# Window attention in one pass on one core: second scores one step later, rings of seven for the maxima, softmax sums spread by VectorE

## What is computed

```python
x = conv(quantize(min(1, |x|)), sign(W) * mean|W|) + b
# attention over 7x7 = 49 regions of 8x8 = 64 tokens, 8 heads of 8, the 4 best regions for each
qkv = layernorm(x) @ wqkv + bqkv
idx = top_k(mean(q) . mean(k), 4)                     # per region
kg, vg = k[idx], v[idx]                               # 4 x 64 = 256 keys
attn = softmax(q @ kg.T / sqrt(8)) @ vg
x = x + attn @ wo + bo
x = x + gelu(layernorm(x) @ w1 + bm1) @ w2 + bm2
```

## Time and profile before

| what | value |
|---|---|
| median of 3 runs | 5555.56 us (5546.46 to 5559.63) |
| the profiled execution | 5569.85 us, its span 5568.0 us |
| mean granted TensorE clock | 0.909 |
| TensorE busy | 4677.0 us, 84% |
| VectorE busy | 3447.6 us, 62% |
| ScalarE busy | 3285.4 us, 59% |
| GpSimd busy | 2747.0 us, 49% |
| transfers | 487.33 MB in 627124 packets, 88 GB/s |

### The profile page before, as it was taken

The page is one execution under the profiler, slowest core; times in us unless marked ns, Lnnn a source line. Parts: engine busy times, 40 slices in busy tenths (PEclk is TensorE's granted clock), DMA queues, the critical chain, the costliest instruction groups (busy, mean ns, idle before and its releaser), DMA issues.

```text
span 5568.0 us, 230234 instructions
## 1 busy us (share of the span) xinstructions
PE 4677.0 (84%) x68754; PEld 3217.0 (58%) x68754; DVE 3447.6 (62%) x7969; ACT 3285.4 (59%) x6282; POOL 2747.0 (49%) x9656
## 2 busy tenths in 40 slices
PE   2388888888889888888888888888888888888888
PEld 1265565656556565565656656565565656556564
DVE  2266666666666666666666666666566666667665
ACT  1156556565665656556565665656556565665656
POOL 1245455454544545445454554545455454554553
PEclk8589999998998999889989999989899999989999
DMA  1333343333333333333333423333343333323311
GB/s 53 102 98 92 83 109 76 100 77 96 102 77 98 84 95 91 82 103 80 94 83 91 111 72 103 81 96 92 79 109 79 96 81 102 100 75 102 84 40 33
DMA packets 627124, 487.33 MB, mean 88 GB/s; under 512 B 483792, under 2 KB 613968, under 8 KB 615536
## 3 DMA queue, kind: packets, MB, share of 16 engines
q10 hardware_dynamic: 335360, 205.62, 16.4%
q1 hardware_dynamic: 290416, 265.73, 16.2%
HBM read 262.38 MB, written 208.73 MB: 85 GB/s over the span
## 4 chain that ended last, share of the span: by engine, by line
PE 45%; DMA 18%; issue 10%; SPq 7%; ACT 7%; DVE 5%; DVEq 3%; POOL 2%; ACTq 2%; POOLq 1%
DMA max_d<-tr 11%; PE ps L988 9%; PE ps L1002 7%; PE ps L1019 7%; PE ps L881 4%; DMA qm<-qk_d 3%; PE ps L938 3%; DMA xin<-in_x 3%; DVEq L223 2%; DVE mx L724 2%; SPq L327 2%; PE ps L949 2%; PE ps L901 2%; ACT hid L813 2%; PE ps L974 2%
## 5 line engine op out<-in xcount | busy, mean ns | idle before, releaser
L724 DVE TENSOR_REDUCE mx<-ps 128x4 f32<-128x1024 f32 x1568 | 1921.7, 1226 | 1702.3 <-PE ps L988 1354.0
L832 ACT ACTIVATE pt<-ps 128x512 f32<-128x512 f32 x3136 | 1694.3, 592 | 869.2 <-PE ps L1002 814.4
L506 POOL COPY vg<-vs 64x64 f32 x6272 | 1526.5, 243 | 782.0 <-POOL kg L490 576.7
L988 PE MATMUL ps<-kg,qm 96*128 96x256 f32 x6272 | 1336.2, 338 | 386.6 <-DVE mx L724 127.3
L490 POOL CAST kg<-ks 96x128 fp32r x3136 | 851.0, 297 | 1511.6 <-PE ps L1002 1156.6
L988 PEld LDWEIGHTS ps<-kg,qm 96*128 96x128 f32 x6272 | 946.8, 202 | 1053.6 <-issue 889.5
L1002 PE MATMUL ps<-qm,kg 97*128 97x256 f32 x6272 | 1119.8, 301 | 178.8 <-ACT pt L832 102.3
L1019 PE MATMUL ps<-pt,vg 128*32 128x64 f32 x50176 | 1091.4, 231 | 0.0
L1002 PEld LDWEIGHTS ps<-qm,kg 97*128 97x128 f32 x6272 | 926.2, 203 | 252.2 <-ACT pt L832 164.8
L1019 PEld LDWEIGHTS ps<-pt,vg 128*32 128x32 f32 x50176 | 826.1, 115 | 224.2 <-issue 34.8
L643 DVE CAST kg<-ks 96x128 fp32r x3136 | 625.6, 241 | 126.2 <-issue 123.5
(11 more groups left out here) (109 smaller groups left out, 3866.7 us busy)
## 6 DMA issues: line engine op xcount, KB each, us to landing
qk_d<-stg SPq DMA_DIRECT2D x224, 448.0 KB
qm<-qk_d ACTq DMA_DIRECT2D x1792, 42.0 KB
ks<-qk_d ACTq DMA_DIRECT2D x96, 784.0 KB, 6.2
vs<-v_d ACTq DMA_DIRECT2D x64, 784.0 KB, 6.7
xin<-in_x SPq DMA_DIRECT2D x119, 224.0 KB
xi_d<-xi SPq DMA_DIRECT2D x112, 224.0 KB
qk_d<-stg SPq DMA_DIRECT2D x112, 224.0 KB
max_d<-tr SPq DMA_DIRECT2D x1568, 2.0 KB
```

What stands on the lines that cost most here:

```text
L506: j = pool.tensor_copy(dst.rearrange("p j (e x) -> p j e x", e=2)[:, :, :, 0:HD], vs[place(m)[0]][rows, bass.ds(region, 1), :].rearrange(" ...
L724: v.tensor_reduce(mx[h % 2][:].rearrange("p (g j e) -> p g j e", g=2, j=2)[:, :, :, 0], ps[:, 0:2, :].rearrange("p g (j k) -> p g j k", j= ...
L832: act.activation(pt[m % 2][:, c], ps[:, 2 + c, :], ACT.Exp, scale=float(HD) ** -0.5).then_inc(S["pt_ready"], 1)
L988: i = pe.matmul(ps[:, g, 256 * j:256 * j + 256], qm[c % 2][0:NP3, t, g, 2 * j:2 * j + 2, :].rearrange("p h t -> p (h t)"), kg[slot][0:NP3, ...
```

## The change

- `ST_LAG` 3 to 4 and `PV_LAG` 4 to 5; `LEAD`, `P_AT`, `F_AT` and `ROUTE_AT` one step later. `X_AT`, `A_LOAD` and `B_LOAD` stay.
- `mx`, `tr` and `hopped` become rings of seven. VectorE's wait for a free buffer moves from the maximum to the transpose and asks for the hop of seven steps before.
- SyncE first issues the store of step h, then the read-back of step h-2.
- `pick` and its matmuls go. VectorE spreads the sums with `stream_shuffle` at offsets 0 and 1 of the finish, into `rc`, and ACT's logarithm reads `rc`. The waits that guarded PSUM banks 5 and 6 go to later matmuls.
- The queries of the next seven steps are loaded in steps 4 and 5 of each seven, four transfers each.

```diff
+SPREAD = [24] * HD + [25] * HD + [24] * 16
-ST_LAG = 3
-PV_LAG = 4
+ST_LAG = 4
+PV_LAG = 5
-LEAD = 18
+LEAD = 19
-P_AT, P_EVERY = 18, 6
-F_AT, F_EVERY = 60, 7
+P_AT, P_EVERY = 19, 6
+F_AT, F_EVERY = 61, 7
-ROUTE_AT = 62
+ROUTE_AT = 63
...
-        mx = [sb(f"mx{i}", [128, 32]) for i in range(2)]
-        tr = [sb(f"tr{i}", [128, 32]) for i in range(2)]
+        mx = [sb(f"mx{i}", [128, 32]) for i in range(RING)]
+        tr = [sb(f"tr{i}", [128, 32]) for i in range(RING)]
...
-            if t in (3, 4, 5) and live((c + 1) * NW, kind):
+            if t in (ST_LAG, ST_LAG + 1) and live((c + 1) * NW, kind):
-                if t == 3 and not (kind == "lead" and c < 1):
+                if t == ST_LAG and not (kind == "lead" and c < 1):
                     eng.wait_ge(S["st_full"], (p * STEPS + c * NW) * 2)
-                queries(eng, p + (c + 1) // 14, (c + 1) % 14, [(g, h) for g in range(NG) for h in range(HG)][(t - 3) * 3:(t - 2) * 3])
+                queries(eng, p + (c + 1) // 14, (c + 1) % 14, [(t - ST_LAG, h) for h in range(HG)])
...
-                m = h - 1
+                if live(h, kind):
+                    sp.wait_ge(S["tr_ready"], T + 1)
+                    sp.dma_start(max_d[h % RING].rearrange("j (b n) -> b j n", n=32), tr[h % RING][0:128:8, :]).then_inc(hopped[h % RING], 16)
+                m = h - 2
                 if live(m, kind):
-                    sp.wait_ge(hopped[m % 2], (p * R + m // 2 + 1) * 16)
+                    sp.wait_ge(hopped[m % RING], (p * 14 + m // RING + 1) * 16)
                     sp.dma_start(qm[m // NW % 2][NP3:NP3 + 1, m % NW].rearrange("o g h t -> o (g h t)").bitcast(F32),
                                  max_d[m % RING].rearrange("j p -> (j p)").unsqueeze(0)).then_inc(row_ready[m % RING], 16)
-                if live(h, kind):
-                    sp.wait_ge(S["tr_ready"], T + 1)
-                    sp.dma_start(max_d[h % RING].rearrange("j (b n) -> b j n", n=32), tr[h % 2][0:128:8, :]).then_inc(hopped[h % 2], 16)
...
+                    if off in (0, 1):
+                        if off == 0:
+                            v.wait_ge(S["um_ready"], p * (4 * 14) + (NW + s + 1) * 4)
+                        v.stream_shuffle(rc[:, off], um0[:, s] if off == 0 else um1[:, b], SPREAD).then_inc(S["sum_full"], 1)
...
-                    if live(h - 2, kind):
-                        v.wait_ge(hopped[h % 2], (p * R + (h - 2) // 2 + 1) * 16)
-                    v.tensor_reduce(mx[h % 2][:].rearrange(...
+                    v.tensor_reduce(mx[h % RING][:].rearrange(...
...
+                    if live(h - RING, kind):
+                        v.wait_ge(hopped[h % RING], (p * 14 + h // RING) * 16)
                     v.wait_ge(S["mx_ready"], T + 1)
-                    v.transpose(tr[h % 2][:], mx[h % 2][:]).then_inc(S["tr_ready"], 1)
+                    v.transpose(tr[h % RING][:], mx[h % RING][:]).then_inc(S["tr_ready"], 1)
...
-                        act.activation(rc[:, i], ps[:, 5 + i, 0:ST], ACT.Ln).then_inc(S["lns_ready"], 1)
+                        act.activation(rc[:, i], rc[:, i], ACT.Ln).then_inc(S["lns_ready"], 1)
...
-                    if off == 0:
-                        pe.wait_ge(S["um_ready"], p * (4 * 14) + (NW + s + 1) * 4)
-                        if s >= 2:
-                            pe.wait_ge(S["ot_ready"], 1 + n - 1)
-                        elif kind == "loop":
-                            pe.wait_ge(S["l_ready"], (p + 2) * (2 * NW))
-                            pe.wait_ge(S["v_ready"], (p + 2) * NW)
-                        if s:
-                            pe.wait_ge(S["lnv2_ready"], n)
-                        for i, src in enumerate((um0[:, s], um1[:, s % 2])):
-                            pe.matmul(ps[:, 5 + i, 0:ST], pick[:], src, start=True, stop=True).then_inc(S["sum_full"], 1)
                     if off == 4:
                         pe.wait_ge(S["un_ready"], n * 2 + 2)
                         if s:
                             pe.wait_ge(S["z_ready"], n * 2)
+                        elif kind == "loop":
+                            pe.wait_ge(S["l_ready"], (p + 2) * (2 * NW))
+                            pe.wait_ge(S["v_ready"], (p + 2) * NW)
...
                     if off == 9:
                         pe.wait_ge(S["nm2_ready"], n + 1)
-                        if s < NW - 1:
-                            pe.wait_ge(S["lns_ready"], n * 2 + 4)
+                        pe.wait_ge(S["ot_ready"], 1 + n)
+                        if s == 0 and kind == "loop":
+                            pe.wait_ge(S["lg_ready"], p + 2)
```

More of the change, by code:

```diff
@@ L110, in build @@
         ident = sb("ident", [128, 128])
-        pick = sb("pick", [128, 128])
         mean_w = sb("mean_w", [128, 128])
@@ L177, in build @@
         idx_loaded = [sem(f"idx_loaded{i}") for i in range(2)]
-        hopped = [sem(f"hopped{i}") for i in range(2)]
+        hopped = [sem(f"hopped{i}") for i in range(RING)]
         row_ready = [sem(f"row_ready{i}") for i in range(RING)]
@@ L908, in route @@
                     pe.wait_ge(S["l_ready"], q * (2 * NW) + 2 * NW)
-                    if not first:
-                        pe.wait_ge(S["lns_ready"], p * (2 * NW) + 1)
                     settled(pe)
```

17 lines of the change are left out of this document (6 added, 11 removed).

## The result

The changed kernel takes 5805.75 us in the median (5788.79 to 5838.42) against 5555.44 (5546.46 to 5559.63) of the kernel before in the same comparison: a ratio of 1.046, with a 95% interval from 1.0409 to 1.0511. It is slower by about 250 us, 16 us for each of the 16 pairs. The forecast was 5380 us and a range up to 5540; the direction was wrong.

The account below looks back on a forecast made before the run. PE was taken to bound the quiet steps, waits followed by half-clock steps the others. Terms of -0.7, -5.0, -4.5, -2.0, 0 and +1.0 made -11.2 us a pair, -176 with the ends: 5380 us, range 5250 to 5540.

Parts of the forecast that it names:

- The term of the query loads: Batches of four on ACT's queue: near nothing in quiet cycles, +1.0 us a pair in all, bounds -2 and +5.
- so it starts about 0.6 sooner: Last query batch: two more loads add 0.84 us, but no merge copy is ahead, so it starts 0.6 us sooner.
- PE idles into the low clock: Rival: without `pick`, PE's pauses in quiet cycles bring half clock, about 1.4 us more a cycle, 5540 us; chance 0.05.
- lag and order: Strip steps: read-back stalls of 6.5 us a pair against the hop wait removed; sum 0, bounds -6.7 and +9.
- the whole worth of the hop wait: The 30 strip steps: 87.3 us less 80.6 busy on PE, 6.7 us a pair, set against the read-back stalls.
- late read-back: Rival: second scores in strip items wait for the read-back, 2.8 us in each of seven items, 5590 us; chance 0.13.
- the gain in the loaded steps: Steps with key and value loads: the maximum no longer waits for a hop, -4.5 us a pair, between 0 and 8.
- about 10: The 12 steps with key and value loads: us lost a pair against the quiet pace and the loop's turn.
- the 17 later steps: Steps behind the first finish: rings give -2.0 us a pair of an excess of 8.6.
- The shuffle: VectorE's pass in place of `pick`: 0.63 us each and 0.1 for its pattern; quiet cycles -0.7 us a pair.
- The first finish: First strip's finish: the `pick` matmuls, their 2.67 us wait and slow matmuls behind leave the path, -5.0 us a pair.
- bare steps above 2.3: Sign of error: bare steps longer than 2.3 us, where the timeline before showed a cycle of 2.22.

Follow-up runs that it names:

- y2: Query loads in two batches of four, in steps 4 and 5, alone on the kernel before: 5766.19 us, ratio 1.0435.
- w1: The changed kernel with query loads 3, 3 and 2 in steps 3, 4 and 5, as before: 5629.63 us, ratio 1.0129.
- x3: The changed kernel with the `pick` matmuls back, no shuffle, and `mx` at two buffers: 5783.75 us, ratio 1.0416.
- x4: The changed kernel with unread matmuls added in the two steps that lost the `pick` matmuls: 5753.22 us, ratio 1.0369.
- v1: The changed kernel with queries 3, 3, 2 in steps 3 to 5 and the read-back of h-1 behind the store of h: 5429.32 us, ratio 0.9767.
- u2: The changed kernel with queries 3, 3, 2, read-back of h-1 behind the store, and unread matmuls in the steps without `pick`: 5360.29 us, ratio 0.9648.
- x2: Sums by shuffle in place of the `pick` matmuls, alone on the kernel before: 5489.71 us, ratio 0.9899.
- x1: Rings of seven for `tr` and `hopped`, alone on the kernel before: 5519.24 us, ratio 0.9943.
- w2: The changed kernel with queries 3, 3, 2 in steps 3 to 5 and SyncE's old order: 5480.43 us, ratio 0.9862.
- z1: Rings of seven for `tr` and `hopped` and the shuffle, together on the kernel before: 5459.52 us, ratio 0.9887.
- v2: The kernel before with rings and shuffle, and queries four and four in steps 2 and 3: 5454.74 us, ratio 0.9819.
- w3: The kernel before with rings and shuffle, and queries 3, 3, 2 a step earlier, in steps 2 to 4: 5387.11 us, ratio 0.9703.

## Why the prediction was wrong

**The term of the query loads failed most.** The sum held +1.0 a pair, bounds -2 and +5. On the kernel before the edit costs 4.35 points (y2), 15 us a pair; taking it back from the change gives 3.3 points (w1), 11.5 a pair. The step that failed is "+0.84, [...] so it starts about 0.6 sooner", which led to "near nothing in quiet cycles". The cycle's end in the timeline of after, steps 5, 6 and 0:

```profile
2986.36 1.81 ACTq L238 DMA_DIRECT2D qm<-qk_d  x4
2987.41 0.99 PE L979 MATMUL ps<-kg,qm 96*128 96x256 f32 x4
2988.28 0.58 ACT L781 ACTIVATE xin<-xin 128x448 f32<-128x448 f32 x1 [1.79 <-issue]
2988.77 0.62 ACT L798 ACTIVATE st<-ps,made 128x448 f32<-128x448 f32 x1
2989.41 0.58 ACT L800 ACTIVATE st<-st 128x448 f32<-128x448 f32 x1
2989.76 0.31 ACTq L238 DMA_DIRECT2D qm<-qk_d  x1
2989.81 0.71 PE L979 MATMUL ps<-kg,qm 96*128 96x256 f32 x4 [0.35 <-DVE mx L722]
...
2990.23 0.32 ACTq L238 DMA_DIRECT2D qm<-qk_d  x1
...
2990.70 0.84 ACTq L238 DMA_DIRECT2D qm<-qk_d  x2
...
2993.29 0.71 PE L979 MATMUL ps<-kg,qm 96*128 96x256 f32 x4 [1.19 <-DMA qm<-qk_d]
2993.84 0.64 PE L993 MATMUL ps<-qm,kg 97*128 97x256 f32 x4
2994.41 0.65 PE L1010 MATMUL ps<-pt,vg 128*32 128x64 f32 x32
2995.00 1.02 PE L960 MATMUL ps<-nm,w 64*128 64x448 f32 x4
```

And the same steps of the kernel before:

```profile
2885.68 0.98 PE L988 MATMUL ps<-kg,qm 96*128 96x256 f32 x4
...
2887.92 0.31 ACTq L237 DMA_DIRECT2D qm<-qk_d  x1
...
2888.39 0.31 ACTq L237 DMA_DIRECT2D qm<-qk_d  x1
...
2890.73 0.50 PE L988 MATMUL ps<-kg,qm 96*128 96x256 f32 x2
```

Counted from the first scores of step 5, the first load of the last batch goes out at 2.24 before (2885.68 to 2887.92) and at 2.35 after: no 0.6 gained, since three activations of other work, themselves late by the 1.79 us of issue in step 4, stand ahead of it on ACT. The last issue ends at 3.02 before (2888.70) and at 4.13 after (2991.54). I had put the end 0.2 later; it came 1.1 later. And I took the time between the last issue and PE's need for slack. There was none: in this cycle the 1.1 us became 1.19 us of wait. Over the run PE waits for queries at 130 of the 224 starts of seven steps, 2.0 us each, where it was 44. The most is at step 77, where loads of keys and values are in flight as well: in pairs 2 to 14, 5.3 us in each pair, where the kernel before waited 2.7 us in 10 of the 13.

**Then the clock.** A query wait at the end of two steps without `pick` is often followed by half-speed steps. The example, from the timeline of after, opens the second line of the table of stretches; its granted clock is 0.50 from 2698.48 to 2703.00:

```profile
2698.48 1.19 PE L979 MATMUL ps<-kg,qm 96*128 96x256 f32 x4 [3.15 <-DMA qm<-qk_d]
2699.47 1.05 PE L993 MATMUL ps<-qm,kg 97*128 97x256 f32 x4
2700.46 1.08 PE L1010 MATMUL ps<-pt,vg 128*32 128x64 f32 x32
2701.47 1.87 PE L960 MATMUL ps<-nm,w 64*128 64x448 f32 x4
```

The step takes 1.19, 1.05, 1.08 and 1.87 where the step from 2993.29 above, behind a wait of 1.19, takes 0.71, 0.64, 0.65 and 1.02 at clock 1.00. So not every wait does it. I counted, in pairs 2 to 14, the first steps of each seven that ran over half of their time at the lower clock, by the query wait ahead of them:

| query wait | after | x3, after with `pick` | x4, after with unread matmuls | v1 | u2, v1 with unread matmuls |
|---|---|---|---|---|---|
| under 1 us | 2 of 13 | 6 of 24 | 4 of 22 | 0 of 2 | 0 of 5 |
| 1 to 2 us | 34 of 45 | 17 of 35 | 23 of 43 | 10 of 15 | 6 of 22 |
| over 2 us | 47 of 47 | 29 of 33 | 36 of 36 | 27 of 27 | 19 of 20 |

Behind the waits of 1 to 2 us the bare steps matter; behind longer ones the clock fell with work in them too. Over the run the first MLP matmuls (L960, L969 before), which stand just there, have a mean of 915 ns against 631 before. The time at the lower clock rose from 1013 to 1533 us. This is the rival "PE idles into the low clock", which I gave 0.05 because the quiet stretch of the earlier trace rows kept clock 1.00 in spite of pauses. The evidence was right as far as it went, and x2 mostly bears it out: without `pick` and without a longer wait the clock is some 0.008 lower. I had not asked what the bare steps and one of the waits would do together. Filling the bare steps gives back 0.9 points (x4) and 1.2 points (u2), some 50 to 65 us, a fifth to a quarter of the loss. That is not the whole price of the clock: the added matmuls take PE's time themselves, and behind the long waits they do not help. The Trainium skill ("TensorE: Matmul & The Clock Gate", HAM oscillation) had the sign right: the mean granted clock fell from 0.909 to 0.868.

**The term "lag and order" failed next.** It stood at 0 with an upper bound of +9. w1 against v1, which differ only in h-2 or h-1, are 3.6 points apart, 12.7 us a pair by the medians and 9.8 by the traces. The mechanism was the one that I described, a read-back with 1.9 us left to land. In the timeline of after, strip steps of the seventh pair (SPq is SyncE's queue):

```profile
2853.53 0.54 SPq L364 DMA_DIRECT2D max_d<-tr  x1
...
2854.28 0.82 SPq L370 DMA_DIRECT2D qm<-max_d  x1
...
2856.50 0.73 PE L993 MATMUL ps<-qm,kg 97*128 97x256 f32 x4 [0.57 <-DMA qm<-max_d]
...
2857.93 0.59 SPq L364 DMA_DIRECT2D max_d<-tr  x1
2858.63 0.38 SPq L370 DMA_DIRECT2D qm<-max_d  x1
...
2860.59 0.74 PE L993 MATMUL ps<-qm,kg 97*128 97x256 f32 x4 [1.16 <-DMA qm<-max_d]
```

Issue to use is 2.22 and 1.96 us, and PE waits 0.57 and 1.16 of it. What was mis-sized are three things. I set the whole worth of the hop wait, 6.7 us a pair, against it as if it came free: but x1 gives 1.7 in these steps. Each stall also lowers the clock: w1's strips are 6.8 us longer than v1's and spend 6.2 us more at half clock. Matmuls take 1.6 to 1.8 times as long there in the two steps compared above, so by an estimate some 2.5 of the 6.8 are slow work and not waiting. And both grown waits feed each other: in the strip steps the query batches alone cost nothing (y2 87.6 against 88.7), the late read-back alone 6.9 (w1), both together 12.0 (after). w1 and after have rings, shuffle and lag besides.

**Rings: the gain in the loaded steps did not come.** The sum held -4.5 a pair for them. With the 13 steps compared as in the table, they went from 54.7 to 54.4 with rings alone (x1) and to 54.6 in the change. They reach 52.9, -1.8, in v1 (lag of four, store first, read-back of h-1), where neither hop nor read-back makes PE wait for long; in the old order they take 54.5 with that lag (w2) and 55.7 without it (z1). So the rings free VectorE, and only then do the read-back and the queries show as PE's waits. The excess itself was misread: of the "about 10" lost in steps 7 to 18, 3.5 us are the first strip's convolution in step 18, which is work. For the 17 later steps I took -2.0; the rings gave -0.4, and the change +5.7, with the query wait in them.

**What was right.** The shuffle takes 655 ns (0.63 taken), its pattern next to nothing. The group of after:

```profile
L695 DVE STREAM_SHUFFLE rc<-um 128x448 f32<-128x448 f32 x224 | 146.6, 655 | 0.0
```

The rate of the Trainium skill ("VectorE: DVE Perf Modes", The perf-mode tier table) gives an estimated 0.53; the measurement is 0.12 above it and decides. The first finish went from 27.0 to 22.7 us a pair, -4.3 for -5.0 predicted. Shuffle alone gives 1.0 point (3.5 us a pair; -5.7 predicted), rings alone 0.6 (2.0; -6.5 predicted). The hop wait left VectorE. The longer lag cost nothing at GpSimd's gathers in the changed kernel: PE waits 31.8 us for them, 37.0 before.

**The signs asked for.** The prediction named as signs of error a read-back wait much more than 73.8 us (its sum held some 110), a query wait above 150, a clock below 1.00 in quiet cycles and bare steps above 2.3. They came as 130.0 us, 265.8 us, 0.92 and, in the cycle shown above, 3.48 us for the bare step from 2989.81, with the 1.19 of query wait in it. The two rivals of the losing side, late read-back and low clock, held together with a third case that had no price of its own, the late queries. Each was priced alone and given 0.18 in sum. The case that decided sat inside the forecast as a small term. It is also why the range failed: its end was set by one rival at a time.

**What stays open.** What carries the 1.2 points between v2 and w3 (ACT's squares are only suspected); why v1 is 0.95 points better than w2; and how u2's order would do with the queries of w3. At four steps of lag the slot of the next queries is read until step 3, so loads in step 2 would need a third slot; this was not tried.

## What to carry to other kernels

Before moving DMA issues onto fewer steps of a computing engine, count them as work of that engine, with everything queued in between, and ask how much slack the consumer of the last one has: here it had none. When a lag is lengthened to give a transfer time, count the steps from its issue to its use after all edits; a reordering that issues it one step later takes back what the lag gave, when it also stands behind another step's store. Removing work from TensorE just ahead of a possible wait has a second price, the clock, so price such edits together and not one by one.

## What the chip showed unexpectedly

- 480 matmuls whose results nobody reads made the kernel 1.2 points faster: clock 0.903 to 0.925, half-speed time 1059 to 806 us.
- Eight DMA issues in a row held ACT for 3.74 us, four for 1.81, three for 1.25; ACT's activations stood still for it.
- Loads in batches of four are slower than 3, 3 and 2 even when all are out a step sooner (0.9819 against 0.9703).
